# A pause after every two groups of gathers on GpSimd, in a recommender tower on one core

## The reference

```
e = stack([tbl_0[ids[:, 0]], ..., tbl_25[ids[:, 25]]], axis=1)      # 512 x 26 x 128
combined = concatenate([dense[:, None, :], e], axis=1)              # 512 x 27 x 128
inter = einsum('bfd,bgd->bfg', combined, combined)[:, iu0, iu1]     # 512 x 351
h = concatenate([dense, inter, dense], axis=1)                      # 512 x 607
h = maximum(h @ W_top1 + b_top1, 0)                                 # 512 x 512
h = maximum(h @ W_top2 + b_top2, 0)                                 # 512 x 256
y = h @ W_top3                                                      # 512 x 1
```

## Time and profile before

| | |
|---|---|
| median of 3 runs | 143.89 us (142.26 to 146.3) |
| the profiled execution's own time | 142.88 us |
| its span, first to last instruction | 141.1 us |
| outside the span | 1.78 us |
| PE busy | 107.9 us (76%) |
| POOL busy | 61.4 us (43%) |
| mean granted TensorE clock | 0.889 of full speed |

### The profile page before, as it was taken

One profiled execution on the slowest core, in us unless ns is written; L12 is line 12 of the kernel. 1 busy time (PEld: TensorE's weight loads), 2 busy tenths in 40 slices (PEclk: granted clock), 3 DMA queues, 4 the chain that ended last, 5 costly groups with the idle time before them and its releaser, 6 DMA issues.

```text
span 141.1 us, 3365 instructions
## 1 busy us (share of the span) xinstructions
PE 107.9 (76%) x1508; PEld 86.8 (62%) x1508; DVE 67.1 (48%) x98; ACT 42.6 (30%) x64; POOL 61.4 (43%) x63
## 2 busy tenths in 40 slices
PE   5799956999949977336599338346988985999993
PEld 5676835888828744114277237326978965889981
DVE  0799999819995244633174008000360254139210
ACT  3425391193940105700070614101041401201120
POOL 2677788787878787787356005730000000000000
PEclk9999999999999999985557996555589999999999
DMA  3995999742999111222101000210000000000000
GB/s 93 335 380 156 344 278 358 281 129 58 352 314 262 48 50 37 56 60 56 37 16 40 19 5 23 55 38 5 5 5 5 0 5 7 5 0 0 5 0 1
DMA packets 5683, 13.83 MB, mean 98 GB/s; under 512 B 1838, under 2 KB 1838, under 8 KB 5668
## 3 DMA queue, kind: packets, MB, share of 16 engines
q1 hardware_dynamic: 3732, 9.67, 20.3%
q0 software_dynamic: 1792, 3.67, 9.4%
q10 hardware_dynamic: 144, 0.26, 0.8%
HBM read 13.60 MB, written 0.00 MB: 96 GB/s over the span
## 4 chain that ended last, share of the span: by engine, by line
PE 46%; issue 20%; POOL 17%; DMA 7%; DVE 6%; another core or an unknown queue 2%; ACT 1%; DVEq 0%
POOL xg L262 17%; PE prod L446 10%; PE acc L395 6%; PE acc L394 6%; PE acc L480 6%; DMA xg<-table,gids 5%; PE flip L429 4%; PE acc L491 4%; DVE oh L330 3%; PE acc L462 3%; DMA gids<-gather_ids 2%; PE flip L480 2%; PE acc L502 2%; DVE tl L323 2%
## 5 line engine op out<-in xcount | busy, mean ns | idle before, releaser
L262 POOL DMA_INDIRECT xg<-table,gids x56 | 60.6, 1082 | 31.0 <-issue 16.2
L394 PE MATMUL acc<-oh,th 128*128 128x512 f32 x96 | 43.1, 449 | 9.3 <-DVE oh L330 4.7
L330 DVE TENSOR_SCALAR oh<-tab_ids,rowno 128x1024 fp32r<-128x1024 int16 x48 | 34.4, 760 | 19.7 <-PE acc L395 9.0
L395 PE MATMUL acc<-oh,tl 128*128 128x512 f32 x96 | 41.2, 429 | 0.2 <-issue 0.2
L394 PEld LDWEIGHTS acc<-oh,th 128*128 128x128 f32 x96 | 20.0, 209 | 17.8 <-issue 8.8
L395 PEld LDWEIGHTS acc<-oh,tl 128*128 128x128 f32 x96 | 20.2, 211 | 6.1 <-issue 2.6
L446 PE MATMUL prod<-xT 128*32 128x27 f32 x1024 | 14.1, 206 | 12.9 <-issue 12.9
L446 PEld LDWEIGHTS prod<-xT 128*32 128x32 f32 x1024 | 12.2, 122 | 15.8 <-issue 15.4
L296 ACT COPY xT<-flip 128x512 f32<-128x512 f32 (+1 forms) x16 | 9.8, 628 | 39.5 <-PE flip L429 22.4
L291 ACT COPY xT<-acc 128x512 f32<-128x512 f32 x12 | 13.5, 1249 | 15.5 <-PE acc L395 9.7
L323 DVE TENSOR_TENSOR tl<-tab,th 128x1024 fp32r<-128x1024 f32 (+1 forms) x15 | 14.7, 1011 | 5.7 <-PE acc L395 3.0
(11 more groups left out here) (38 smaller groups left out, 59.2 us busy)
## 6 DMA issues: line engine op xcount, KB each, us to landing
tab<-onehot_tables SPq DMA_DIRECT2D x11, 512.0 KB
tab_ids<-onehot_ids SPq DMA_DIRECT2D x5, 256.0 KB
xg<-table,gids POOLq DMA_INDIRECT x56
w1z_sb<-w1z SPq DMA_DIRECT2D x1, 702.0 KB
tab<-onehot_tables SPq DMA_DIRECT2D x2, 256.0 KB, 4.0
w1d_sb<-w1d SPq DMA_DIRECT2D x1, 512.0 KB
w_sb<-w SPq DMA_DIRECT2D x1, 512.0 KB
tab_ids<-onehot_ids ACTq DMA_DIRECT2D x1, 256.0 KB, 3.7
```

What stands on the lines that cost most here:

```text
L262: pool.indirect_dma_start(xg[:, q % XG_RING, s - lo, :], None, tables[s - 1], bass.IndirectOffsetOnAxis(ap=gids[:, n:n + 1], axis=0)).then ...
L330: nc.vector.tensor_scalar(oh[:, n % OH_RING, :], tab_ids[:, p % IDS_RING, :], rowno[:, j:j + 1], None, ALU.is_equal).then_inc(oh_ready, 1)
L394: nc.tensor.matmul(out_i, th[:, p % 2, i, j, :], one, start=(j == 0), stop=False)
L395: return nc.tensor.matmul(out_i, tl[:, p % 2, i, j, :], one, start=False, stop=(j == R - 1))
```

## The change

Before group 2, 4, 6, 8, 10, 12 and 14, GpSimd now also waits until all gathers of the group before have landed. A semaphore counts the landings in one buffer, so the wait is for the second of the two groups last issued. Nothing else differs: the same transfers in the same order into the same buffers, and the same lists on the other engines.

```diff
 XG_RING = 6
+REST = 2
 OH_RING = 8
...
             for q in range(TILES * NC_T):
                 t, (lo, hi) = q // NC_T, CHUNKS[q % NC_T]
+                if q and q % REST == 0:
+                    pool.wait_ge(xg_in[(q - 1) % XG_RING], 16 * gathers_through(q - 1))
                 if q >= XG_RING:
                     pool.wait_ge(flipped, FLIPS["chunk", q - XG_RING])
                 for s in range(lo, hi):
```

## The result

The changed kernel takes 154.23 us (median of four runs, 152.78 to 154.98) against 145.09 us (142.26 to 148.27): a ratio of 1.077, 95% interval 1.058 to 1.096. It is slower; 145.4 us was forecast, in a range of 136 to 154. The profiled execution took 152.78 us with a span of 150.9 us, 9.8 us above the span of before.

What follows compares the result with a forecast made beforehand. TensorE was taken as the bound, busy 107.9 of 141.1 us, with slow issue while gathers are in flight. 10.4 us of late flips, mostly regained, left +2.5 us at the end: 142.88 + 2.5 = 145.4 us, range 136 to 154.

Steps and rivals of the forecast that it cites:

- The waits and the late flips: GpSimd's new waits, 1.4 to 6.7 us each by loading, delay TensorE's flips: 10.4 us late behind group 7.
- The relief in the one-hot stage: Twelve one-hot steps behind group 7: pauses speed 8.2 steps, stage ends at 79.2 us; of 10.4 us late, 1.3 left.
- the crawl: All engines issue slowly while gathers are in flight; 16.3 us lost in the one-hot steps, again in tile 1's products.
- The products: tile 0 as before: Small matmuls of tile 0 after the one-hot stage: cost unchanged, group 8 flipped only 1.3 us later.
- The last gathers against tile 1: Products of tile 1: last gather lands 6.3 us later, 3.8 us regained after a pause, so +2.5 us at the end.
- the crawl has nothing to do with gathers: Rival, all engines: pauses give nothing back, all 10.4 us from the flips stay, 153.3 us (149 to 157); chance 0.28.
- The quick landing: Rival, GpSimd's waits: gathers land sooner with fewer queued, pauses 1.4 us each, no flip waits, 138.0 us; chance 0.08.
- The pauses end the crawl for good: Rival, behind group 7: 10.4 us late less 16.3 us of loss, 137.0 us (133 to 141); chance 0.22.
- the sign set down for it: Step from group 7 to the one-hot stage's end, 27.3 us before: near 11 us would mean the slow issue is gone.

Runs made afterwards that it cites:

- rests_2_4: Changed kernel with the new waits only before groups 2 and 4: 157.17 us beside 146.25 us of the kernel before.
- rests_late: Changed kernel with the new waits only before groups 10, 12 and 14: 142.84 us beside 145.8 (ratio 0.990); again, 144.95 beside 146.25.
- no_late: Kernel before without the 28 gathers of groups 8 to 15, their flips rereading buffers of groups 4 to 7: 126.55 us beside 145.8.
- ring10: Kernel before with ten gather buffers in place of six and no new waits: 158.78 us beside 145.8.
- rest_8: Changed kernel with only the new wait before group 8: 125.13 us beside 125.14 of the kernel before, ratio 1.003.
- after_third: The changed kernel unaltered, run again beside the kernel before in a group at the lower time level: 134.9 us beside 125.07, ratio 1.074.

## Why the prediction was wrong

*The waits and the late flips: right.* Rests of 6.6 us under loading and 1.8 us later stand against 6.7 and 1.4; the two between them, 2.4 and 3.5 us, against 3 and 5.6. Group 4 waited 7.15 us where 6.4 were laid out (45.0 against an arrival at 38.6). The wait of group 6 that had been laid out did not come, and the rest before it was 2 us shorter than taken. TensorE was 8.5 us late behind group 7 instead of 10.4. In the free trace this lateness is nearly all of the cost.

*The relief in the one-hot stage: right in kind, too small.* I took 3.8 steps to crawl and the stage to end at 79.2 us. None crawled: 11.3 us for twelve steps, end at 71.3. With the rests before 6 and 8 taken away (rests_2_4) the crawl is back at 27.6 us. That fits these rests giving the relief, and so does the table; but the two runs of rests_late, where the crawl came early by itself, have the same 11.3 us without them. So what the rests spare is the crawl before the stage's end, wherever it would have fallen, and not a fixed loss behind group 7.

*"The products: tile 0 as before": this step failed.* It cost 20.5 us instead of 7.1, 13.4 us more. Before, those products had run while GpSimd waited from 76.94 to 85.96 us for the flip of group 8; the last gather had been issued before the stage began. My own layout put the issue of groups 12 and 13 at 80.5 to 90.5 us (measured: 78.70 to 88.40), right beside these products, and I priced a crawl only for tile 1. I had found a cost that goes with gathers, moved the gathers, and left a stage at its old price. That the gathers beside this stage are its cost is shown by the table: without them 7.1 to 7.7 us in five traces, 12.8 us where they overlap in part. With the stage at its measured 20.5 us the sum would have been 13.4 us higher, less the 7.9 us by which the one-hot stage ended earlier than laid out: about 151 us, against the 152.78 of the profiled execution.

*The last gathers against tile 1: right within 2 us.* The last gather was issued by 100.9 us against 99.4 laid out, and the stage from group 8 to group 12 was 1.6 us longer than before; +1.2 had been forecast for it. The last 1.4 us are behind group 12, where the matmuls of the top layer (L483) were busy for 10.4 us against 8.7 before, a stretch of them at a lower granted clock (0.6 in the slice near 125 us).

*The rivals.* The one called "the crawl has nothing to do with gathers" gave 153.3 us, close to the 154.23 measured, by a mechanism that the runs refute for crawling groups: no_late has no crawl, ring10 has more of it, and tile 0 crawls as long as gathers run beside it. That its number came so close is luck. Its sum (late flips and nothing else) is what happens in free groups: 10.4 us by the layout, 9.8 measured. What the runs do not refute is its other half, that the engines' own supply of instructions is what is slow, held up in some way by the gathers; no trace names a releaser. Part of the stops is there without gathers: before the first product of tile 0 TensorE stands for 2.31 us in no_late as in the kernel before. The quick landing is refuted by the 6.61 us rest. "The pauses end the crawl for good" held for one stage only, although the sign set down for it, a step near 11 us from group 7, came true: a sign taken in one stage said nothing of the next.

*Two readings in the prediction are wrong.* The crawl of the kernel before did not begin near 40 us in its trace: the flip at 47.10 us and the steps behind it are at full pace, and the first stop is the 0.89 us before 51.50. And GpSimd's stop before 71.73 us is at gather 47, the first of group 13, which is none of the seven places of the new waits. Neither enters the sum.

*What is shown and what not.* Shown: in a free group the late flips are nearly the whole cost. In crawling groups the late gathers are needed for the crawl, and with the rests before 6 and 8 the one-hot stage ends without one, while the gathers that they push back make the products of tile 0 crawl by 13 to 15 us. Whether the late flips still add to the time there depends on where the crawl of the kernel before fell: 8.5 us in one pair of traces, none in the other. That the two kinds of groups give nearly the same difference, 8 to 10 us, is a coincidence of sums (8.5 - 15.2 + 13.4 + 3.0 in the first pair) and not one cause. Not shown: why the crawl exists in some groups and not in others, since free groups have the same gathers; by what way gathers slow the engines, and whether it takes the transfers or GpSimd's issuing of them; that holding groups 12 and 13 would have freed tile 0; whether plain transfers crawl too. No version here beats the kernel before: rests_late (0.990) and rest_8 (1.003) cannot be told from it.

## What to carry to other kernels

A cost found in one stage must be charged in every stage to which the edit moves its cause: lay out where the moved work lands, and price each stage beside it anew. A pause put into an in-order queue to help others is free only where nobody waits for what is behind it, and beside heavy loading it lasts as long as a loaded landing (2.4 to 6.6 us here), not an idle one (1.8 us). And before a stall without a releaser is charged to a change, the unchanged kernel should be seen in several groups of runs: here it was there or not there, 20 us apart.

## What the runs showed of the hardware

- The kernel before has two levels, about 145 us and 125 us, by the group of runs; the same chip had both. The 28 late gathers cost nothing that shows at the lower level: without them no_late took 126.55 us, no less, though in a crawling group.
- In the crawl TensorE, VectorE and ScalarE are slow together and GpSimd keeps its pace, but for one stop of 3.08 us at its end in the kernel before: with gathers in an unbroken row (ring10), 23 matmuls in 31 us on TensorE and one stop of 28.11 us on ScalarE, beside 25 gathers, at a DMA share of 0.19.
- In crawling groups the small matmuls of one tile took 7.1 to 7.7 us without gathers beside them and 20.5 to 22.0 us with 14 to 18.5 us of gathers; in a free group 7.2 us with five gathers beside them (after_third).
- A gather of 128 rows of 512 bytes holds GpSimd for 1.8 us from the end of its issue to the next issue when it is waited for, table loads being over, and 2.4 to 6.6 us beside them.
- GpSimd fills of 128x1024 raised VectorE's one-hot instruction from 0.76 to 0.96 us in the mean.
